# Four cross-attention blocks on one core: the norms' scaling and the heads' shares go from VectorE to GpSimd, and the stages are dealt anew

## What is computed

```python
def attention(q_in, kv_in, kind):                  # kind: window of 64, causal, or all keys
    s = einsum("bhqd,bhkd->bhqk", q(q_in), k(kv_in)) * scale + mask
    return softmax(s) @ v(kv_in) @ Wo + bo

def layernorm(x, g, b, eps=1e-5):
    m, v = mean(x), var(x)
    return (x - m) / sqrt(v + eps) * g + b

# block 0: norm(x + attention(window)); norm(x + attention(ctx)); norm(x + gelu(x W1) W2)
# block 1: the same with a causal attention; block 2: norms of x and ctx first, silu, no norm behind;
# block 3: norm(x + attention(ctx)), the output
```

## Time and profile before

| | us |
|---|---|
| median of 3 runs | 3474.37 (3473.01 to 3484.79) |
| the profiled execution, its own time | 3478.41 |
| its span, first to last instruction | 3476.1 |
| PE busy | 3287.5 (95%) |
| DVE busy | 2669.1 (77%) |
| ACT busy | 2171.3 (62%) |
| POOL busy | 1705.7 (49%) |

### The profile page before, as it was taken

The page is one execution under the profiler, slowest core; times in us unless marked ns, Lnnn a source line. Parts: engine busy times, 40 slices in busy tenths (PEclk is TensorE's granted clock), DMA queues, the critical chain, the costliest instruction groups (busy, mean ns, idle before and its releaser), DMA issues.

```text
span 3476.1 us, 57660 instructions
## 1 busy us (share of the span) xinstructions
PE 3287.5 (95%) x20152; PEld 1782.9 (51%) x20436; DVE 2669.1 (77%) x6523; ACT 2171.3 (62%) x2823; POOL 1705.7 (49%) x1497
## 2 busy tenths in 40 slices
PE   7999899999999999999999999999999999999998
PEld 5555545544555644554454565554446456455443
DVE  5976997766896698776799669777688966977667
ACT  3565666666666666666656656666575665666665
POOL 6634644444663464443475345444457544544442
PEclk9999999999999999999999999999999999999999
DMA  7312321223321231122343122112233312212221
GB/s 226 116 62 79 110 79 62 83 71 104 122 91 53 89 114 62 62 89 68 110 129 104 55 93 87 59 59 89 80 119 121 103 63 86 83 52 81 68 65 53
DMA packets 304449, 304.23 MB, mean 88 GB/s; under 512 B 52050, under 2 KB 278226, under 8 KB 302226
## 3 DMA queue, kind: packets, MB, share of 16 engines
q1 hardware_dynamic: 278436, 298.18, 26.9%
q10 hardware_dynamic: 25728, 2.36, 0.6%
HBM read 217.60 MB, written 82.84 MB: 86 GB/s over the span
## 4 chain that ended last, share of the span: by engine, by line
PE 72%; DVE 19%; issue 3%; ACT 2%; SPq 1%; POOL 1%; DMA 1%; ACTq 0%; DVEq 0%; another core or an unknown queue 0%; POOLq 0%
PE pv L915 14%; PE mx L867 12%; PE st L890 12%; PE st L564 10%; PE mx L564 10%; PE mx L971 6%; DVE row_max L1149 5%; PE mx L949 3%; DVE mx L1152 3%; DVE y L1220 3%; PE mx L967 2%; ACT probs L1066 1%; DVE normal L1176 1%; DVE st L1209 1%; PE st L986 1%
## 5 line engine op out<-in xcount | busy, mean ns | idle before, releaser
L1066 ACT ACTIVATE probs<-st 128x1024 f32<-128x1024 f32 (+1 forms) x1344 | 1265.5, 977 | 635.7 <-PE st L890 356.5
L1149 DVE TENSOR_REDUCE row_max<-mx 128x1 bf16<-128x512 f32 x2048 | 1288.0, 683 | 203.9 <-PE mx L867 154.0
L1259 POOL TENSOR_TENSOR qm<-q_high,own_rows 128x512 bf16<-128x512 bf16 x768 | 797.6, 1049 | 442.3 <-PE mx L867 299.2
L867 PE MATMUL mx<-k_high,qm 128*128 128x512 bf16 (+4 forms) x2788 | 821.2, 343 | 77.4 <-DVE row_max L1152 25.1
L890 PE MATMUL st<-q_packed,k_packed 97*128 97x512 bf16 (+2 forms) x3072 | 800.4, 345 | 28.9 <-ACT probs L1066 15.1
L915 PE MATMUL pv<-probs,va 128*32 128x512 f32 (+2 forms) x6144 | 704.4, 532 | 5.7 <-ACT probs L1066 3.4
L867 PEld LDWEIGHTS mx<-k_high,qm 128*128 128x128 bf16 x3072 | 270.0, 97 | 694.8 <-DVE row_max L1149 237.5
L890 PEld LDWEIGHTS st<-q_packed,k_packed 97*128 97x128 bf16 (+1 forms) x3072 | 277.3, 98 | 358.0 <-ACT probs L1066 130.9
L1152 DVE CUSTOM_DVE_ANT_0 mx<-mx,tab 128x192 f32<-128x192 f32 (+4 forms) x1024 | 399.2, 442 | 75.2 <-PE mx L867 62.0
L1287 POOL TENSOR_TENSOR rstd<-spread_of,m_half 128x2 f32<-128x2 f32 x144 | 99.9, 694 | 466.0 <-DVE spread_of L1214 464.0
L1276 POOL TENSOR_TENSOR xl<-xT,xh 128x512 fp32r<-128x512 f32 x116 | 149.5, 1289 | 228.1 <-ACT xh L1034 227.6
(11 more groups left out here) (119 smaller groups left out, 4762.3 us busy)
## 6 DMA issues: line engine op xcount, KB each, us to landing
k_packed<-k_parts_dram SPq DMA_DIRECT2D x576, 128.0 KB, 2.7
q_packed<-q_parts_dram SPq DMA_DIRECT2D x576, 128.0 KB, 2.6
q_parts_dram<-q_low SPq DMA_DIRECT2D x96, 256.0 KB, 2.2
k_parts_dram<-k_low SPq DMA_DIRECT2D x96, 256.0 KB, 2.2
raw_w<-squares_dram SPq DMA_DIRECT2D x69, 256.0 KB, 2.9
q_parts_dram<-q_high SPq DMA_DIRECT2D x48, 256.0 KB, 2.1
k_parts_dram<-k_high SPq DMA_DIRECT2D x48, 256.0 KB, 2.1
raw_w<-w_dram SPq DMA_DIRECT2D x48, 256.0 KB, 2.9
```

The costliest lines, as they stand in the source:

```text
L867: mm = pe.matmul(bank[:, 0:k1 - k0], qm[:, h % RING, i * P:(i + 1) * P], high["k"][s][:, t, k0:k1], start=True, stop=True)
L1066: act.activation(dst[:, :, 0:w], held["scores", b, a, n, e][:, :, 0:w], ACT.Exp, scale=ATT_SCALE[a]) \
L1149: ins = dve.tensor_reduce(top, scores, AX_X, ALU.max, negate=True)
L1259: pool.tensor_tensor(qm[:, h % RING], high["q"][s][:, h // HT], own_rows[:, h % HT:h % HT + 1].to_broadcast([P, TOK]), ALU.mult) \
```

## The change

1. GpSimd instead of VectorE adds the norms' epsilon (now `L1283`), does both instructions of `scale` (`L1292`) and the heads' shares (`L1277`). The stage list within each stream stays: only the engine is another, and the waits follow (`turn` waits on GpSimd's semaphore, `oT` and the next `turned` wait for GpSimd's shares).
2. Before the exponential ScalarE's wait for `scores` stands first and the one for `values` of two steps before second.
3. All 14 strings of `MERGE` are new. Each string has as many of each digit as before, since the stages are the same.

```diff
@@ -331,36 +331,36 @@
 MERGE = {
...
-    "21": "110012001112001101124111013132101111022121011410141201102320421110211140112211011110102122001010"
-           "11021102010232220222202013222020202020222020200222022020022020220020",
...
+    "21": "101200102311014011301111421010112211221220101100112111401010111011221104141031102120110311011200"
+           "01101222122022201212202200322220020202220220002202220220002220220020",
...
@@ -978,7 +978,7 @@
                     mm.then_inc(*mx_filled.mark(("rows", b, tag, i)))
                 elif kind == "turn":
                     tag, half = stage[2:]
-                    pe.wait_ge(*row_step.past(("scale", b, tag, half)))
+                    pe.wait_ge(*pool_step.past(("scale", b, tag, half)))
                     pair = held["turn", b, tag, half] = st_pair()
                     for j in range(KT):
                         for i in range(2):
@@ -1058,9 +1058,9 @@
                     q0, q1 = span(k_kind, k)
                     w = (q1 - q0) * len(heads) // 2
                     step = LOOP_NO[b, a] * STEPS + n
+                    act.wait_ge(*st_filled.past(("scores", b, a, n, e)))
                     if step >= 2:
                         act.wait_ge(*step_done.nth(step - 1))
-                    act.wait_ge(*st_filled.past(("scores", b, a, n, e)))
                     c = column(k_kind, k, heads[0])
                     dst = probs[:, step % 2, c:c + 2 * TOK].rearrange("p (b n) -> p b n", b=2)
                     act.activation(dst[:, :, 0:w], held["scores", b, a, n, e][:, :, 0:w], ACT.Exp, scale=ATT_SCALE[a]) \
@@ -1165,22 +1165,16 @@
                     t, odd = divmod(g, 2)
                     old = (b, a, g - 1) if g else (*before(b, a), NG - 1) if LOOP_NO[b, a] else None
                     blocks = turned[:].rearrange("p (n c) -> p n c", c=BLK)
-                    shares = normal[:].rearrange("p (n c) -> p n c", c=BLK)[:, :, odd * HD:(odd + 1) * HD]
                     dve.wait_ge(*sums_kept.past(("sums", b, a, g)))
                     if old:
-                        dve.wait_ge(*row_step.past(("shares", *old)))
+                        dve.wait_ge(*pool_step.past(("shares", *old)))
                     chain(dve.transpose(turned[:], sums[:, g % 2]), ("turned", b, a, g))
-                    chain(dve.reciprocal(rec[:], blocks[:, :, HD]), ("rec", b, a, g))
-                    if old and not odd:
-                        dve.wait_ge(*row_step.past(("oT", old[0], old[1], old[2] // 2)))
-                    share = dve.tensor_tensor(shares, blocks[:, :, 0:HD],
-                                              rec[:].unsqueeze(2).to_broadcast([P, TOK // BLK, HD]), ALU.mult)
-                    share.then_inc(*row_step.mark(("shares", b, a, g)))
+                    dve.reciprocal(rec[:], blocks[:, :, HD]).then_inc(*row_step.mark(("rec", b, a, g)))
                     if odd:
                         if LOOP_NO[b, a] and not t:
                             pb, pa = before(b, a)
                             dve.wait_ge(*mx_filled.past(("add", pb, "a4", KT - 1) if pa == 4 else ("rows", pb, f"a{pa}", TT - 1)))
-                        dve.wait_ge(*row_step.past(("shares", b, a, g)))
+                        dve.wait_ge(*pool_step.past(("shares", b, a, g)))
                         dve.transpose(oT[:, t], normal[:]).then_inc(*row_step.mark(("oT", b, a, t)))
                 elif kind == "rows":
                     tag, i = stage[2:]
@@ -1210,21 +1204,12 @@
                     chain(ins, ("stats", b, tag, half))
                     for i in (2 * half, 2 * half + 1):
                         ins = dve.bn_aggr(moments[:, i, :], st6[:, i, :])
-                    chain(ins, ("moments", b, tag, half))
-                    dve.tensor_scalar(spread_of[:, at], moments[:, at, 1], EPS, None, ALU.add) \
-                        .then_inc(*row_step.mark(("eps", b, tag, half)))
-                elif kind == "scale":
-                    tag, half = stage[2:]
-                    dve.wait_ge(*pool_step.past(("rstd", b, tag, half)))
-                    for i in (2 * half, 2 * half + 1):
-                        ins = dve.tensor_scalar(y[:, i, :], y[:, i, :], moments[:, i, 0:1], rstd[:, i:i + 1],
-                                                ALU.subtract, ALU.mult)
-                    ins.then_inc(*row_step.mark(("scale", b, tag, half)))
+                    ins.then_inc(*row_step.mark(("moments", b, tag, half)))
                 elif kind == "out" and b + 1 == B:
                     half = stage[3]
                     ys = y[:, 2 * half:2 * half + 2]
                     g7, b7 = (rv(n).unsqueeze(1).to_broadcast([P, 2, D]) for n in ("g7", "b7"))
-                    dve.wait_ge(*row_step.past(("scale", b, "a5", half)))
+                    dve.wait_ge(*pool_step.past(("scale", b, "a5", half)))
                     chain(dve.tensor_tensor(ys, ys, g7, ALU.mult), ("g7", b, half))
                     dve.tensor_tensor(ys, ys, b7, ALU.add).then_inc(*row_step.mark(("out", b, half)))
 
@@ -1280,17 +1265,38 @@
                     pool.wait_ge(*act_step.past(("m", b, a, m)))
                     pool.tensor_tensor(low[m][:, 1], rest[m][:], low[m][:, 0], ALU.subtract) \
                         .then_inc(*pool_step.mark(("l", b, a, m)))
+                elif kind == "heads":
+                    a, g = stage[2:]
+                    t, odd = divmod(g, 2)
+                    old = (b, a, t - 1) if t else (*before(b, a), NG // 2 - 1) if LOOP_NO[b, a] else None
+                    blocks = turned[:].rearrange("p (n c) -> p n c", c=BLK)
+                    shares = normal[:].rearrange("p (n c) -> p n c", c=BLK)[:, :, odd * HD:(odd + 1) * HD]
+                    pool.wait_ge(*row_step.past(("rec", b, a, g)))
+                    if old and not odd:
+                        pool.wait_ge(*row_step.past(("oT", *old)))
+                    pool.tensor_tensor(shares, blocks[:, :, 0:HD], rec[:].unsqueeze(2).to_broadcast([P, TOK // BLK, HD]), ALU.mult) \
+                        .then_inc(*pool_step.mark(("shares", b, a, g)))
                 elif kind == "stats":
                     tag, half = stage[2:]
                     at = slice(2 * half, 2 * half + 2)
-                    pool.wait_ge(*row_step.past(("eps", b, tag, half)))
+                    pool.wait_ge(*row_step.past(("moments", b, tag, half)))
+                    pool.tensor_scalar(spread_of[:, at], moments[:, at, 1], EPS, None, ALU.add) \
+                        .then_inc(*pool_step.mark(("eps", b, tag, half)))
+                    pool.wait_ge(*pool_step.past(("eps", b, tag, half)))
                     pool.tensor_tensor(rstd[:, at], spread_of[:, at], m_half[:, at], ALU.pow) \
                         .then_inc(*pool_step.mark(("rstd", b, tag, half)))
+                elif kind == "scale":
+                    tag, half = stage[2:]
+                    pool.wait_ge(*pool_step.past(("rstd", b, tag, half)))
+                    for i in (2 * half, 2 * half + 1):
+                        ins = pool.tensor_scalar(y[:, i, :], y[:, i, :], moments[:, i, 0:1], rstd[:, i:i + 1],
+                                                 ALU.subtract, ALU.mult)
+                    ins.then_inc(*pool_step.mark(("scale", b, tag, half)))
                 elif kind == "out" and b + 1 < B:
                     half = stage[3]
                     ys = y[:, 2 * half:2 * half + 2]
                     g7, b7 = (rv(n).unsqueeze(1).to_broadcast([P, 2, D]) for n in ("g7", "b7"))
-                    pool.wait_ge(*row_step.past(("scale", b, "a5", half)))
+                    pool.wait_ge(*pool_step.past(("scale", b, "a5", half)))
                     pool.tensor_tensor(ys, ys, g7, ALU.mult).then_inc(*pool_step.mark(("g7", b, half)))
                     pool.wait_ge(*pool_step.past(("g7", b, half)))
                     pool.tensor_tensor(ys, ys, b7, ALU.add).then_inc(*pool_step.mark(("out", b, half)))
```

56 lines of the change are left out of this document (28 added, 28 removed).

## The result

| | us |
|---|---|
| before, median of the runs beside it | 3476.82 (3473.01 to 3484.79) |
| after, median of 4 runs | 3553.86 (3552.43 to 3557.11) |
| after / before | 1.022, 95% interval 1.0199 to 1.0241 |

The change makes the kernel 2.2% slower. The forecast was 3400 us, range 3310 to 3465.

What follows compares the result with a forecast made beforehand. TensorE, busy 95%, looked like the bound, stopped often and briefly by VectorE. The terms, -80 - 10 + 5 + 15 - 5 = -75 us, took the profiled 3478.4 to 3403, as median 3400 us; range 3310 to 3465.

Steps and rivals of the forecast that it cites:

- second term: Before `turn` in the norms: VectorE's queue goes, GpSimd's latencies come; a gain of 10 us, bounds -90 and +128.
- first term: TensorE's waits for VectorE's row maxima: half of a 160 us loss goes, -80 us, bounds 0 and -160.
- slower rival: Norm's scalings, epsilon and power one behind another on GpSimd keep TensorE before `turn`: about 3525 us, chance 0.08.
- list of signs: Expected in the profile after: DVE busy near 2330 us, POOL 2000 to 2210, loads waiting for maxima about 200.
- Third and fourth term: Heads' shares slower on GpSimd: +5 us; GpSimd's masks and low parts late: +15 us, bounds 0 and +60.
- Fifth term: ScalarE's exponential, its wait for `scores` now on itself, starts 0.06 us sooner: -5 us, 12 at most.
- The cover: TensorE's products before `turn`: nearly 8 us behind a feed-forward; 3.3 behind an attention, against a path of 4.2.

Runs made afterwards that it cites:

- The line of three points: Changed kernel with only the scaling's instruction on GpSimd varied: pairs of 1.18, 1.83 and 2.44 us gave 3411, 3481 and 3554 us.
- The product: Changed kernel with each scaling as one tensor_tensor of y and broadcast rstd, mean not subtracted: 3410.82 us; the same under the old strings: 3683.57 us.
- The probe: Kernel before with 27 GpSimd instructions added at its end, three of each of nine forms; the scaling's form at 256 numbers took 1218 ns.
- the versions with divided scaling: Changed kernel with one row of each pair on VectorE, one on GpSimd: 3474.07 us; with rows placed by half and norm: 3466.38 us.

## Why the prediction was wrong

**The step that failed** is in the second term, "The turns": "2 x 0.65", with the upper bound "850 at the most". The upper bound of 850 ns a scaling, and the 650 taken, stood for 1229: outside the bound, and the path grew by 1.16 us a pair over what was taken. The line of three points shows that this is the cause, and its size: from 1.3 to 2.44 us of pair it is 3424 to 3554, 130 of the 154 us by which the forecast missed. The product, with 613 ns a row, runs in 3411 and is almost the forecast, waits for `L1292` included (23.6 us of matmuls, 57.5 of loads, 50 to 110 expected; after: 127.2 and 167.5). Where the 24 us left belong isn't shown; the first term, below, came out smaller by at least as much.

Why the bound didn't hold: it came from `xl` and `k_low`, which are TENSOR_TENSOR. I took a TENSOR_SCALAR with two operations for cheaper, since it streams one input. The probe shows the opposite, 1218 against 722 ns at the same size. The fixed part and slope of one form didn't carry over to the other. The prediction also weighed a rule of the Trainium skill (GPSIMD Engine Reference, Engine selection) against the change: GpSimd is about twice as slow with two inputs. It took 0.82 us for the scaling from this, but the scaling streams one input, and of one input the same row says "1-input is roughly line-rate". The trace doesn't agree with that: the scaling takes 3.0 times VectorE's median (1229 against 408 ns). The shares, with two inputs, take 1.5 times VectorE's (622 against 426), less than twice.

**The slower rival** is what happened, nearly as written: "decides from about 1.1 us a scaling", "about 3525" at 1.3. It had a chance of 0.08 only because of the bound. At 1.23 its own sum, 96 x 1.16 - 75, is +36; the runs give +77. Its sum took the -75 whole, of which the first term's 80 wasn't there in full, and it had neither the wait that is told next nor the clock.

**What no step had**: the wait ahead of `scale` 1 in GpSimd's queue. I counted "one `cl`" or a mask ahead by its length (1.05 us), not by what it waits for. The run with `scale` 1 ahead of `low` 0 gives 52 us back. The two overlap: with `scale` 1 ahead, TensorE's idle time before `turn` 1 is down to 16.2 us, near the 10.3 of the product's run, so the 52 are not to be added to the 130. Without this wait and with the long pair the kernel is still at 3502, slower than before.

**First term, the maxima, -80**: the size was off, by about half or more. VectorE went to 2368 us (2332 forecast, 2330 in the list of signs) and has no stretched lump left, but the loads wait 305.6 us (about 200 forecast), in the product's run 297.6. The matmuls wait 31.8 in place of 49.3. Between these two views, the time from the start of one matmul to the start of the next, beyond the usual, falls by some 40 us at the maxima, an estimate from the start times in the traces that doesn't part the causes. So lumps weren't the main thing that made maxima late, and the prediction had named this as what would be wrong then. What else makes them late is open.

**Third and fourth term, shares +5, masks +15**: the shares' duration was over-estimated, and VectorE's own wait for them, with the maxima queued behind it, was left out. `oT` waits for GpSimd 89.8 us in the kernel after:

```profile
DVE oT L1178 <- POOL normal L1277: 89.8, 92, 4.2
```

Under the new strings the shares on GpSimd gain 10 us in all even so (measured with the scaling divided), under the old they cost. Loads waiting for `qm` are 26.4 us, no more than before, where they were 29.3 before, so the fourth term is nearer to 0. The row of before:

```profile
PEld mx L867 <- POOL qm L1259: 29.3, 43, 0.8
```

In the window stretch GpSimd is busy 116.41 of 143 us, 81% where 85% was forecast, while the stretch itself grew from 133:

```profile
867.00:1010.00 143.00, 130.18 (x1055) 78.88 (x1060) 102.28 (x386) 87.82 (x117) 116.41 (x112) 0.96 0.33 104
```

POOL's busy time came to 2190 against 2114: the scalings gave 164 us more (351.3 - 288 x 0.65), shares and epsilons 68 less, and the other lines the 20 less that are left.

**Fifth term, the swapped waits, -5**: right, 0.14% less time and a start 0.03 us behind the product.

**The cover.** "Behind a feed-forward that has cover" held, `f1` half 0 has no idle time before `turn`. The new strings were taken as free. They cost 46 us on the kernel before. Of this, 32 us are new waits at `turn` (66.7 against 35.2): they count on a `scale` that doesn't stand behind VectorE's copies. The sum had no term for this.

**Open.** Why the versions with divided scaling stop at 3474 and 3466, when TensorE's idle time before `turn` (58.3 and 35.9 us) is down to less than half and to little more than a quarter of after's 127.8. The product's run has 24.2 there and is 56 us faster than the better of them, so `turn` explains 12 of these; the maxima wait longer too (48.0 us of matmuls against 18.3), and the rest isn't shown. Why scaling alone (3776) and the product (3684) cost what they do under the old strings, beyond the wait that was moved, the shares and the clock. Whether other strings would hide a pair of 2.44 us wasn't tried.

## What to carry to other kernels

Before work moves to another engine, take its price from the same form of instruction there (operations, scalars from memory, broadcast), and where no row has it, let the upper bound reach past every other form's row, or run a few of it as a probe. In a queue that works in order, ask of each instruction ahead of the moved one what it waits for, not only how long it takes. An order written by hand fits one length of path on one engine: a move and its order are to be judged together, since each alone was slower here, and both together were 2% faster with a pair of 1.2 us (with the mean left out) and 2.2% slower with one of 2.4.

## What the runs showed of the hardware

- GpSimd, 128x256 f32: two operations with scalars from memory 1218 to 1229 ns, with constants 1072; one operation 923 to 928, with a constant 847; two whole inputs 722, with a broadcast second input 612. At 512 numbers the first takes 2072. A broadcast second input was cheaper than a whole one.
- Two numbers a partition still take 230 ns (epsilon) and 719 (power) on GpSimd.
- With the scaling and shares gone from VectorE its lumps of up to 2242 and 2339 ns are gone as well. What was stretched was 100 us of busy time, yet TensorE's loads still wait 305.6 us for maxima, of 326.4. On GpSimd the scaling isn't stretched: 1210 to 1246 ns over all 288.
- ScalarE's exponential starts 0.04 us behind its product in the median when the wait that ends last is on the instruction itself, 0.10 when it is a separate one ahead of it.
- The mean granted clock was lower in the kernels in which TensorE waited more: 0.994 before, 0.985 after, 0.943 with the old strings. That is 42, 104 and 439 us at 1.2 GHz. With the pair at 1.18, 1.83 and 2.44 us and nothing else changed it is 37, 70 and 104 us, so part of what a longer wait costs comes with the clock.
